# Two depthwise convolutions on one core: where ScalarE issues its four stores among conv 1's images

## The chip, the cores and the metric

The kernel runs on one core of a Trainium2 chip. Its time is the device time of one execution in microseconds, the median of three runs. A core has five engines with a queue of instructions each: TensorE (PE), VectorE (DVE), ScalarE (ACT), GpSimd (POOL) and SyncE (SP). They run side by side and wait for each other through semaphores. Transfers are done by 16 DMA engines, whichever engine issues them. Here SyncE issues loads, ScalarE issues stores and GpSimd and SyncE issue copies within the on-chip memory.

## The reference

```python
def _gn(v, G=32, eps=1e-5):                      # 384 channels in 32 groups of 12
    g = v.reshape(B_, G, C_ // G, H_, W_)
    m = jnp.mean(g, axis=(2, 3, 4), keepdims=True)
    s = jnp.var(g, axis=(2, 3, 4), keepdims=True)
    return ((g - m) / jnp.sqrt(s + eps)).reshape(v.shape)

x = x + depthwise_conv(_gn(x), L0_conv_k)        # 3 x 3, padding 1
w = (w + rot90(w, 1) + rot90(w, 2) + rot90(w, 3)) * 0.25
x = x + depthwise_conv(_gn(x), w)                # 7 x 7, padding 3
```

x is (8, 384, 128, 128) in float32.

## The kernel before

A **unit** is one group of 12 channels of four images, and a **chunk** is four of its channels; three chunks make a unit, and there are 64 units and 192 chunks. The rows of an image lie on the 128 partitions. A chunk passes through a software pipeline: every engine runs `slot(t)` for one t after another, and in a slot it works on several chunks at different stages. The order on each engine is the order in which `slot` is written; only semaphores tie the engines together. Slots repeat in threes, as a unit has three chunks.

In both convolutions, an image is split into a high part and a low part in float16. ScalarE writes the high part of the first normalisation into H1 (L551) and the whole value in float32 into Z (L554), and GpSimd subtracts the one from the other for the low part (L656). TensorE then multiplies with banded matrices (L731), and VectorE adds the result to X and takes its sum (L483). For the second normalisation GpSimd writes the high part into H2 (L635), ScalarE the whole value into the same Z (L534), and VectorE the low part (L466). The rows of H2 have to be gathered into overlapping blocks of rows, BT: GpSimd issues the high gather (L648), SyncE the low one (L238, L240), and VectorE copies the high block once more (L504). TensorE runs conv 2 on BT (L764), and VectorE adds its result to X (L447) and gives `out_done`. ScalarE stores X (L565).

Z has one place for each of four images, and both normalisations use it: L551 of image `img` waits in `normalise1` until L466 has read the older chunk's Z of that image (`lo_done[1]`).

In slot t, ScalarE does in this order: the four L534 of chunk t-4; then L551 and L554 of chunk t+1, image by image, with the store of chunk t-6 of the same image behind each; then `square(t)`, four times L577, which waits for L483 (`y_done`). Only the first of a slot's four stores waits (`out_done`, in `store` with `img == 0`); the others need nothing more. In every third slot TensorE sums over the partitions behind this (L693): it waits for all squares of the unit (`squared`). The sums of the first layer are L703.

VectorE does in slot t: L447 of chunk t-6, the four L466 of chunk t-4, the statistics of a loaded chunk (L475), the four L483 of chunk t, L504 of chunk t-4. SyncE does in slot t: four loads for chunk t+5 (L249), which wait until the store of the chunk that had the place before has landed (`stored`), then eight low gathers for chunk t-4. X holds twelve chunks.

The change touches `slot` of ScalarE only; `store` and `normalise1` are as they were.

Of the kernel before, what the change touches and what calls it, by code (L numbers as in the profile page):

```python
# [13 lines left out]
NI = 4  # L14
# [44 lines left out]
def conv_program(nc, x, k1_in, k2_in, out):  # L59
# [18 lines left out]
    with ExitStack() as ctx:  # L78
# [32 lines left out]
        at = [GC * V1 // 2]  # L111
# [56 lines left out]
        def xs(n, img):  # L168

            c = n % CPU_  # L170
            return X[:, ring(n), c * CC:(c + 1) * CC, img, :]
# [6 lines left out]
        def part(H, n, which, img, off, pitch):  # L178
            return H[:, n % 2, which, :, off + img * pitch:off + img * pitch + W]
# [5 lines left out]
        def walk(eng, slot):  # L185

            for t in range(-5, NCH + 7):
                slot(t, lambda n: n)

        def wait_apart(eng, semaphore, value):  # L190


            eng.wait_ge(semaphore, value)
            if not isinstance(value, int):
                eng.sem_inc(passed, 1)
# [3 lines left out]
        def real(n):  # L199
            return 0 <= n < NCH  # L200
# [321 lines left out]
        @block.scalar  # L522
        def _(act):
            def normalise2(n, at):

                m = NI * at(n)
                rb = RB[:, 1, (n // CPU_) % 2]
                for img in range(NI):

                    if real(n + 4):  # L530
                        act.wait_ge(lo_done[0], m + 4 * NI + img + 1)
                    else:
                        act.wait_ge(lo_done[1], m - NI + img + 1)
                    nc.scalar.activation(Z[:, img, :].rearrange("p (c w) -> p c w", c=CC), xs(n, img),  # L534
                                         ACT.Identity, bias=rb[:, 1, img:img + 1],
                                         scale=rb[:, 0, img:img + 1]).then_inc(normed[1], 1)

            def normalise1(n, img, at):

                m = NI * at(n)  # L540
                rb = RB[:, 0, (n // CPU_) % 2]
                if img == 0:
                    if n == 0:
                        act.wait_ge(zeroed, 9)
                    if n >= 2:
                        wait_apart(act, conv1_done, at(n) - 1)
                if real(n - 5):
                    act.wait_ge(lo_done[1], m - 5 * NI + img + 1)
                elif n > 0:
                    act.wait_ge(lo_done[0], m - NI + img + 1)  # L550
                nc.scalar.activation(part(H1, n, 0, img, O1, P1), xs(n, img), ACT.Identity,  # L551
                                     bias=rb[:, 1, img:img + 1],
                                     scale=rb[:, 0, img:img + 1]).then_inc(hi_done[0], 1)
                nc.scalar.activation(Z[:, img, :].rearrange("p (c w) -> p c w", c=CC), xs(n, img),  # L554
                                     ACT.Identity, bias=rb[:, 1, img:img + 1],
                                     scale=rb[:, 0, img:img + 1]).then_inc(normed[0], 1)

            def store(n, img, at):

                c, half = n % CPU_, (n // CPU_) % HALVES  # L560
                ch0 = (at(n - n % GCH) // GCH) * GC + c * CC
                if img == 0:
                    wait_apart(act, out_done, at(n) + 1)
                dst = out[half * NI + img, bass.ds(ch0, CC), :, :].rearrange("c h w -> h c w")
                act.dma_start(dst, xs(n, img)).then_inc(stored[n % BODY], 16)  # L565

            def take_root(layer, u):
                act.wait_ge(fin[layer], u * FIN + 4)
                nc.scalar.activation(TMP[:, layer, 3], TMP[:, layer, 2], ACT.Sqrt).then_inc(root[layer], 1)  # L569

            def square(n, at):

                for img in range(NI):
                    act.wait_ge(y_done, NI * at(n) + img + 1)
                    if n > 0 or img >= 2:
                        act.wait_ge(squared, NI * at(n) + img - 1)
                    nc.scalar.activation(DUMP[:, img % 2].rearrange("p (c w) -> p c w", c=CC), xs(n, img), ACT.Square,  # L577
                                         accum_out=SS[:, n % CPU_, img, 1:2]).then_inc(squared, 1)

            def slot(t, at):  # L580
                n = t - 4
                if real(n):
                    if n % CPU_ == 0:
                        act.wait_ge(fin[1], (at(n) // CPU_) * FIN + FIN)
                    normalise2(n, at)
                n = t - 3
                if real(n) and n % CPU_ == 0:
                    take_root(1, at(n) // CPU_)
                n = t + 1
                if real(n) and n % CPU_ == 0:  # L590
                    act.wait_ge(fin[0], (at(n) // CPU_) * FIN + FIN)
                for img in range(NI):
                    if real(t + 1):
                        normalise1(t + 1, img, at)
                    if real(t - 6):
                        store(t - 6, img, at)
                if real(t):
                    square(t, at)
                n = t + 2
                if real(n) and n % CPU_ == 0:  # L600
                    take_root(0, at(n) // CPU_)

            walk(act, slot)


# [184 lines left out]
```

## Time and profile before

| | us |
|---|---|
| median of three runs | 3197.03 |
| lowest and highest run | 3193.38, 3197.71 |
| profiled execution, its own time | 3199.24 |
| its span, from the first to the last instruction | 3197.4 |
| TensorE busy in the span | 2858.9 |
| VectorE | 2726.5 |
| GpSimd | 2201.2 |
| ScalarE | 2155.5 |

The profiled execution is one execution. Busy time counts arithmetic only; an issue of a transfer is not in it. In the rows below an engine's name with a q behind it, such as ACTq, means its sequencer, which issues transfers, and PE is TensorE's array. A row's duration of an issue is the time that the sequencer spends on it; the data land later. TensorE's granted clock was 0.968 of full speed in the mean over the span.

### The profile page before, as it was taken

The numbers are of one execution on the slowest core, as the hardware profiler recorded it, in microseconds if no ns is written. First come the engines' busy times: TensorE is split into PE (matmuls) and PEld (weight loads), VectorE is DVE, ScalarE is ACT, GpSimd is POOL, SyncE is SP. The second block draws the span as 40 slices with busy tenths as digits, with TensorE's granted clock in tenths as the row PEclk, the third lists the DMA queues.
The fourth block names the chain that finished last, engine by engine and source line by source line (L and its number), as shares of the span: only waits on it lengthen the run. The fifth ranks groups of instructions, "written<-read, shape, count | busy, mean of one in ns | idle before, by whom it ended". The sixth has DMA issues, their size and how long they took to land.

```text
span 3197.4 us, 76300 instructions
## 1 busy us (share of the span) xinstructions
PE 2858.9 (89%) x28676; PEld 1810.7 (57%) x28676; DVE 2726.5 (85%) x5180; ACT 2155.5 (67%) x3969; POOL 2201.2 (69%) x2321
## 2 busy tenths in 40 slices
PE   0388998999999899999999999999999999989995
PEld 0145565665566565666566666565665565656563
DVE  3377898989899899999899999899898988989885
ACT  1175776777677677777677777677776777767661
POOL 3165776776777677777677777777776777777773
PEclk9798999999999999999999999999999999999997
DMA  2599898888889888989888999888888988988876
GB/s 89 140 234 235 228 237 225 233 225 223 223 237 244 224 223 233 242 234 244 231 233 232 236 234 243 227 232 229 234 231 222 240 236 225 236 229 226 225 181 159
DMA packets 966520, 712.44 MB, mean 223 GB/s; under 512 B 102918, under 2 KB 904710, under 8 KB 966086
## 3 DMA queue, kind: packets, MB, share of 16 engines
q1 hardware_dynamic: 511494, 383.52, 45.8%
q10 hardware_dynamic: 405504, 201.38, 22.5%
q0 software_dynamic: 49152, 122.65, 16.7%
q8 instruction: 227, 3.72, 0.5%
q14 instruction: 143, 1.17, 0.1%
HBM read 259.73 MB, written 220.81 MB: 150 GB/s over the span
## 4 chain that ended last, share of the span: by engine, by line
PE 27%; DVE 23%; POOL 14%; issue 12%; DMA 12%; ACT 5%; SPq 4%; ACTq 2%; DVEq 0%; POOLq 0%
PE PS L731 15%; PE PS L764 11%; POOL H L635 11%; DMA BT<-H 10%; DVE X L483 5%; DVE H L466 5%; DVE BN L475 4%; DVE BT L504 3%; ACT Z L554 2%; ACTq L565 2%; SPq L268 2%; ACT H L551 2%; POOL H L656 2%; POOL BT L648 2%; SPq L238 1%
## 5 line engine op out<-in xcount | busy, mean ns | idle before, releaser
L731 PE MATMUL PS<-H,BAND 128*128 128x512 f16 x6912 | 1567.7, 386 | 78.7 <-DMA BAND<-rows 69.2
L764 PE MATMUL PS<-BT,BAND 118*32 118x512 f16 x21504 | 1277.1, 393 | 129.3 <-issue 98.8
L731 PEld LDWEIGHTS PS<-H,BAND 128*128 128x128 f16 x6912 | 1018.6, 150 | 600.0 <-issue 85.3
L656 POOL TENSOR_TENSOR H<-Z,H 128x512 f16<-128x512 f32 x768 | 840.1, 1096 | 640.7 <-ACT Z L554 639.8
L764 PEld LDWEIGHTS PS<-BT,BAND 118*32 118x32 f16 x21504 | 763.0, 132 | 601.2 <-issue 253.5
L635 POOL TENSOR_SCALAR H<-X,RB 128x512 f16<-128x512 f32 x768 | 894.8, 1174 | 113.3 <-DVE RB L437 78.5
L551 ACT ACTIVATE H<-X,RB 128x512 f16<-128x512 f32 x768 | 619.2, 806 | 436.9 <-DVE H L466 428.5
L554 ACT ACTIVATE Z<-X,RB 128x512 f32<-128x512 f32 x768 | 615.5, 801 | 0.0
L504 DVE COPY BT<-BT 39x8512 f16<-39x8512 f16 x192 | 475.7, 2478 | 161.9 <-DMA BT<-H 158.4
L534 ACT ACTIVATE Z<-X,RB 128x512 f32<-128x512 f32 x768 | 561.4, 803 | 36.2 <-issue 22.0
L577 ACT ACTIVATE DUMP<-X 128x512 bf16<-128x512 f32 x768 | 473.0, 617 | 158.8 <-DVE X L483 156.9
L648 POOL DMA_DIRECT2D BT<-H x768 | 439.1, 577 | 200.2 <-PE PS L764 98.6
L475 DVE BATCH_NORM_STATS2 BN<-X 128x6 f32<-128x512 f32 x768 | 472.5, 675 | 104.9 <-DMA X<-in_x 104.9
L483 DVE SCALAR_TENSOR_TENSOR X<-PS,SC,X 128x512 f32<-128x512 f32 x768 | 528.0, 741 | 30.6 <-PE PS L731 30.3
L466 DVE TENSOR_TENSOR H<-Z,H 128x512 f16<-128x512 f32 x768 | 491.3, 699 | 5.7 <-ACT Z L534 3.4
L447 DVE SCALAR_TENSOR_TENSOR X<-PS,SC,X 128x2048 f32<-128x2048 f32 x192 | 450.2, 2345 | 15.0 <-PE PS L764 12.9
L569 ACT ACTIVATE TMP<-TMP 128x4 f32<-128x4 f32 x128 | 25.6, 200 | 380.6 <-DVE TMP L420 380.6
L577 ACT ACTIVATION_READ_ACCUMULATOR DUMP<-X 128x1 f32 x768 | 143.9, 187 | 0.0
L703 PE MATMUL PS<-MQ,ONES 128*128 128x8 f32 x128 | 25.4, 271 | 64.7 <-DVE MQ L496 64.6
L703 PEld LDWEIGHTS PS<-MQ,ONES 128*128 128x128 f32 x128 | 19.6, 193 | 91.0 <-issue 48.0
L483 DVE DVE_READ_ACCUMULATOR X<-PS,SC,X 128x1 f32 x768 | 61.3, 80 | 0.0
L693 PE MATMUL PS<-SS,ONES 128*128 128x24 f32 x128 | 25.7, 280 | 34.6 <-ACT DUMP L577 34.4
(48 smaller groups left out, 439.6 us busy)
## 6 DMA issues: line engine op xcount, KB each, us to landing
X<-in_x SPq DMA_DIRECT2D x768, 256.0 KB, 5.7
out_y<-X ACTq DMA_DIRECT2D x768, 256.0 KB, 6.7
BT<-H POOLq DMA_DIRECT2D x384, 162.1 KB, 5.2
BT<-H POOLq DMA_DIRECT2D x384, 149.6 KB, 5.6
BT<-H SPq DMA_DIRECT2D x576, 99.8 KB
BT<-H SPq DMA_DIRECT2D x384, 62.3 KB
BT<-H SPq DMA_DIRECT2D x192, 83.1 KB
rows<-v_all SPq DMA_DIRECT2D x8, 1638.0 KB, 11.6
```

Of the source, the lines that this page charges most:

```text
L466: v.tensor_tensor(part(H2, n, 1, img, O2, P2), Z[:, img, :].rearrange("p (c w) -> p c w", c=CC), part(H2, n, 0, img, O2, P2), ALU.subtract ...
L475: v.bn_stats(BN[:, c, img, :], xs(n, img)).then_inc(bn_done, 1)
L483: v.scalar_tensor_tensor(xs(n, img), PA[:, :, img * W:(img + 1) * W], SC[:, 0, bass.ds(g, 1)], xs(n, img), ALU.mult, ALU.add, accum_out=SS ...
L504: v.tensor_copy(BT[AGAIN:AGAIN + WIN, n % 2, :, :, :].rearrange("p b c l -> p (b c l)"), BT[0:WIN, n % 2, :, :, :].rearrange("p b c l -> p ...
L534: nc.scalar.activation(Z[:, img, :].rearrange("p (c w) -> p c w", c=CC), xs(n, img), ACT.Identity, bias=rb[:, 1, img:img + 1], scale=rb[:, ...
L551: nc.scalar.activation(part(H1, n, 0, img, O1, P1), xs(n, img), ACT.Identity, bias=rb[:, 1, img:img + 1], scale=rb[:, 0, img:img + 1]).the ...
L554: nc.scalar.activation(Z[:, img, :].rearrange("p (c w) -> p c w", c=CC), xs(n, img), ACT.Identity, bias=rb[:, 1, img:img + 1], scale=rb[:, ...
L577: nc.scalar.activation(DUMP[:, img % 2].rearrange("p (c w) -> p c w", c=CC), xs(n, img), ACT.Square, accum_out=SS[:, n % CPU_, img, 1:2]). ...
L635: g.tensor_scalar(part(H2, n, 0, img, O2, P2), xs(n, img), rb[:, 0, img:img + 1], rb[:, 1, img:img + 1], ALU.mult, ALU.add).then_inc(hi_do ...
L656: g.tensor_tensor(part(H1, n, 1, img, O1, P1), Z[:, img, :].rearrange("p (c w) -> p c w", c=CC), part(H1, n, 0, img, O1, P1), ALU.subtract ...
L731: last = mm(PA[:, ch, :], band[:, j, ws, :], data[:, :, O1 - 1 + j:O1 - 1 + j + W], start=k == 0, stop=k == 3 * K1 - 1)
L764: last = mm(banks2(n)[b * BL:(b + 1) * BL, ch, :], band[:, j, :], rows, start=j == 0, stop=j == K2 - 1, tile_position=(0, b * BL))
```

## The change

ScalarE no longer issues one store behind each image of conv 1. It issues the stores of images 0 and 1 ahead of the first image, the store of image 2 behind the second image and the store of image 3 behind the fourth.

```diff
@@ -589,11 +589,19 @@
                 n = t + 1
                 if real(n) and n % CPU_ == 0:
                     act.wait_ge(fin[0], (at(n) // CPU_) * FIN + FIN)
-                for img in range(NI):
-                    if real(t + 1):
-                        normalise1(t + 1, img, at)
-                    if real(t - 6):
-                        store(t - 6, img, at)
+                if real(t - 6):
+                    store(t - 6, 0, at)
+                    store(t - 6, 1, at)
+                if real(t + 1):
+                    normalise1(t + 1, 0, at)
+                    normalise1(t + 1, 1, at)
+                if real(t - 6):
+                    store(t - 6, 2, at)
+                if real(t + 1):
+                    normalise1(t + 1, 2, at)
+                    normalise1(t + 1, 3, at)
+                if real(t - 6):
+                    store(t - 6, 3, at)
                 if real(t):
                     square(t, at)
```

ScalarE's queue in one slot before, from the last L534 to the squares. The wait named `lo_done2` is on L466, `out_done` on L447, `y_done` on L483:

```order
L534 ACTIVATE Z<-X,RB 128x512 [waits lo_done1] x3
L551 ACTIVATE H<-X,RB 128x4x128 [waits lo_done2,conv1_done]
L554 ACTIVATE Z<-X,RB 128x512
L565 DMA out_y<-X 128x4x128 [waits out_done]
L551 ACTIVATE H<-X,RB 128x4x128 [waits lo_done2]
L554 ACTIVATE Z<-X,RB 128x512
L565 DMA out_y<-X 128x4x128
L551 ACTIVATE H<-X,RB 128x4x128 [waits lo_done2]
L554 ACTIVATE Z<-X,RB 128x512
L565 DMA out_y<-X 128x4x128
```

Behind it the same three rows come once more for the fourth image, and then the four squares. The same stretch of ScalarE's queue after the change:

```order
L534 ACTIVATE Z<-X,RB 128x512 [waits lo_done1] x3
L565 DMA out_y<-X 128x4x128 [waits out_done]
L565 DMA out_y<-X 128x4x128
L551 ACTIVATE H<-X,RB 128x4x128 [waits lo_done2,conv1_done]
L554 ACTIVATE Z<-X,RB 128x512
L551 ACTIVATE H<-X,RB 128x4x128 [waits lo_done2]
L554 ACTIVATE Z<-X,RB 128x512
L565 DMA out_y<-X 128x4x128
L551 ACTIVATE H<-X,RB 128x4x128 [waits lo_done2]
L554 ACTIVATE Z<-X,RB 128x512
```

The wait for `out_done` and two stores have moved ahead of the first L551; between the second L551 and the third stands one store. The fourth is where it was, ahead of the squares. The order of no other engine changes.

## Rows read from the trace of the kernel before

**Rows 1.** The page's busy times: us busy, share, instructions.

```profile
PE 2858.9 (89%) x28676; PEld 1810.7 (57%) x28676; DVE 2726.5 (85%) x5180; ACT 2155.5 (67%) x3969; POOL 2201.2 (69%) x2321
```

**Rows 2.** Waits of TensorE, 250 to 3120 us: us in total, times, longest.

```profile
PE PS L764 <- issue: 98.8, 31, 13.6
PE PS L693 <- ACT DUMP L577: 29.5, 32, 2.4
PE PS L703 <- DVE MQ L496: 24.1, 19, 2.9
```

**Rows 3.** Chain of waits, 1500 to 1540 us: start, us, what.

```profile
1506.13 5.19 POOL H L635 x4
...
1513.43 9.89 DMA BT<-H
...
1530.13 0.69 DVE H L466
```

**Rows 4.** Timeline of ScalarE: start, us, what, [idle before <- who ended it].

```profile
1526.66 2.93 ACT L534 ACTIVATE Z<-X,RB 128x512 f32<-128x512 f32 x4
1530.93 0.82 ACT L551 ACTIVATE H<-X,RB 128x512 f16<-128x512 f32 x1 [1.34 <-DVE H L466]
1530.98 1.18 ACTq L565 DMA_DIRECT2D out_y<-X  x2
...
1538.95 0.19 ACT L577 ACTIVATION_READ_ACCUMULATOR DUMP<-X 128x1 f32 x1
```

**Rows 5.** Timeline of TensorE, two of its waits.

```profile
1539.19 0.40 PE L693 MATMUL PS<-SS,ONES 128*128 128x24 f32 x2 [1.76 <-ACT DUMP L577]
...
1581.62 8.00 PE L764 MATMUL PS<-BT,BAND 118*32 118x512 f16 x112 [3.39 <-issue]
```

**Rows 6.** Timeline of SyncE ahead of the second of these waits.

```profile
1559.81 7.92 SPq L249 DMA_DIRECT2D X<-in_x  x4
1567.83 0.88 SPq L238 DMA_DIRECT2D BT<-H  x1
...
1575.45 0.71 SPq L240 DMA_DIRECT2D BT<-H  x1
```

**Rows 7.** All instructions of line L565.

```profile
L565 ACTq DMA_DIRECT2D out_y<-X x768: 378/744/4638, 220.9 to 3193.5; - x192
```

**Rows 8.** Timeline of VectorE: the L447 ahead of the L551 above.

```profile
1527.87 2.34 DVE L447 SCALAR_TENSOR_TENSOR X<-PS,SC,X 128x2048 f32<-128x2048 f32 x1
```

**Rows 9.** Timeline of ScalarE: the first two stores of five neighbouring slots.

```profile
1498.10 2.08 ACTq L565 DMA_DIRECT2D out_y<-X  x2
...
1512.01 1.01 ACTq L565 DMA_DIRECT2D out_y<-X  x2
...
1544.50 1.04 ACTq L565 DMA_DIRECT2D out_y<-X  x2
...
1559.03 0.94 ACTq L565 DMA_DIRECT2D out_y<-X  x2
...
1576.41 1.68 ACTq L565 DMA_DIRECT2D out_y<-X  x2
```

**Rows 10.** Timeline of GpSimd behind that slot's images.

```profile
1536.77 1.09 POOL L656 TENSOR_TENSOR H<-Z,H 128x512 f16<-128x512 f32 x1 [0.32 <-ACT Z L554]
1537.84 5.14 POOL L635 TENSOR_SCALAR H<-X,RB 128x512 f16<-128x512 f32 x4
```

**Rows 11.** Waits of VectorE, 250 to 3120 us.

```profile
DVE BT L504 <- DMA BT<-H: 137.2, 81, 4.4
```

**Rows 12.** Table of stretches around two L551; the last but one column is DMA share.

```profile
1511.30:1512.70 1.40, 1.40 (x8) 0.98 (x7) 1.40 (x3) 0.74 (x2) 0.83 (x3) 1.00 0.69 192
1530.20:1531.60 1.40, 1.40 (x17) 0.74 (x19) 1.40 (x4) 0.67 (x1) 0.00 (x0) 1.00 0.87 167
```

**Rows 13.** Waits of ScalarE, 250 to 3120 us.

```profile
ACT H L551 <- DVE H L466: 423.4, 183, 5.8
```

## The prediction

> **What bounds the kernel now.** I read the page's busy times first, then the waits of each engine in the steady part (250 to 3120 us), then the chain of waits over one group of channels, then the timeline of ScalarE where the change is. TensorE is busy 89% of the span [rows 1]; in the steady part its waits come to some 150 us: 98.8 us ahead of conv 2 in 31 places, 29.5 us ahead of the layer-2 sums (L693) in 32 places, 24.1 us ahead of the layer-1 sums (L703) in 19 [rows 2]. The steady part has 61 groups of three chunks, so the L693 wait is there in about half of them. An edit that touches only ScalarE's order can act through these waits and nothing else.
>
> Who sets the L693 wait is seen in the chain [rows 3]. VectorE makes the scale and shift of a unit, GpSimd makes four high parts (L635, 5.19 us), the high gather takes 9.89 us, VectorE copies it (L504), adds conv 2 of an older chunk (L447), makes the low parts (L466), and the first of these frees ScalarE's buffer Z for the first image of conv 1 (L551 at 1530.93). From there ScalarE has eight activations and four squares without a gap: the last accumulator is read at 1538.95 and done at 1539.14 [rows 4], and TensorE, which had idled 1.76 us, starts L693 at 1539.19 [rows 5]. So 8.2 us of ScalarE lie on that path, and a delay of L551 there goes to TensorE one for one whenever the wait is there at all. The 3.39 us ahead of conv 2 at 1581.62 [rows 5] have another cause: SyncE's four loads took 7.92 us to issue from 1559.81, its eight low gathers came only behind them, from 1567.83 to 1576.16 [rows 6], and conv 2 began 5.5 us after the last.
>
> Where the stores stand in this is the point of the case. Today the first two stores are issued from 0.05 us behind the start of L551, not ahead of it: 1530.98, for 1.18 us [rows 4]. During that the activation engine works on what is already queued, so the issue costs nothing, however long. It is often long: 378 ns at least, 744 ns in the median, 4638 ns at most [rows 7].
>
> **The change, part by part.** The number of stores, their bytes and every engine's arithmetic stay. Four things move.
>
> (1) Two stores stand ahead of L551. They wait for `out_done`, which L447 gives at its end, 1530.21 [rows 8]; at this time ScalarE's four L534 are over (1529.59) and its queue is empty [rows 4], so nothing covers the issue. L551 today starts at 1530.93, 0.72 us behind L447. After the change it needs the wait to pass, both issues, and its own dispatch. For wait and dispatch I take 0.15 us, an estimate from the 0.05 us between L551 and the first issue and the 0.11 us between the end of L466 and L551 [rows 3, 4]. For the pair of issues I take what it takes today, in six neighbouring slots: 1.18 us [rows 4] and 2.08, 1.01, 1.04, 0.94 and 1.68 us [rows 9], mean 1.32. The delay of L551 is then 0.15 + 1.32 - 0.72 = 0.75 us, with 0.37 us from the shortest pair and 1.51 us from the longest as bounds. It goes to the path in the 32 places where L693 waits: 32 x 0.75 = +24 us (bounds 12 and 48). In the other groups TensorE comes later than ScalarE, and the delay falls into that slack. So it does in the two slots of a group that have no L693 behind them: TensorE's list names ScalarE at L693 alone [rows 2], since the images that these slots prepare feed a conv 1 that comes a slot later.
>
> At this place a rule of the Trainium skill speaks against my term. The row says that the issue holds ScalarE's sequencer 744 ns in the median [rows 7]. The Trainium skill, page "DMA: Bandwidth & Descriptors", section "Issuing engines are not separate DMA queues", says that the sequencer's time to initiate a DMA "is usually small relative to the DMA itself". By the rule the pair ahead would cost next to nothing, and the sum would lose its first two terms and be -12 us, 3185 us; by the row it keeps them. I go by the row, and the short issue is a rival below.
>
> (2) GpSimd's low parts (L656) follow ScalarE image by image, and the next chunk's L635 starts right behind the last of them (1536.77 + 1.09, L635 at 1537.84) [rows 10]. So the next high gather is issued 0.75 us later too. VectorE waited for a gather's landing in 81 places [rows 11], so a part of them passes the delay on, and TensorE sees it at L703 in 19 places. At most 19 x 0.75 = 14 us, at least nothing; I take a third, +5 us, since only every third gather is of this kind.
>
> (3) The first two stores start some 0.65 us earlier, as L447's end stands 0.72 us ahead of L551. That uses DMA time which is free: the 16 DMA engines are busy 0.69 in the 1.4 us around one such start and 0.87 around another [rows 12]. In the slot whose gather lies on the chain the free share is 0.31, so the saturated stretch behind it becomes 0.65 x 0.31 = 0.2 us shorter. 32 x 0.2 = -6 us; bounds are nothing and the whole shift, 32 x 0.65 = -21 us.
>
> (4) SyncE's loads and low gathers meet the stores 0.65 us earlier. Where the loads are late, as at 1559.81, the stores have gone a little further and the loads come through sooner; where they were early, they now overlap with two stores. 31 stalls, at 0.2 us each as in (3), -6 us; the bounds are the whole shift either way, -20 and +20 us.
>
> The third store is issued behind four dispatched activations and the fourth behind eight, as far into ScalarE's queue as today or earlier. At its place the third store has three activations waiting, some 2.1 us, and the one that runs, 0.8 us (L551's duration in [rows 4]), to hide in; only an issue of over 2.5 us would starve the engine. I cost it at nothing; without the cover it would be some tenths in the few longest cases.
>
> Sum: 24 + 5 - 6 - 6 = +17 us on the profiled execution, whose own time is 3199.24 us: 3216. The median of the runs shown is 3197.03, 2.2 us below the profiled one, so I predict 3214 us.
>
> **Rivals.** *Nothing to be measured.* The time that TensorE loses at L693 is won back by the other waits: while TensorE idles, the DMA engines catch up, gathers land sooner, and the 98.8 us ahead of conv 2 shrink. For this speaks that the DMA engines are nearly full, so every added pause gives them room, and that a shorter pair (0.94 us as in [rows 9]) leaves a first term of 12 us, which (3) and (4) cancel: 12 + 0 - 6 - 6 = 0, 3197 us. Against it: the gather on the chain was issued before the pause, so the pause can't help it.
>
> *Faster.* The stores' start is what matters, not L551: with 1 MB of stores 0.65 us ahead, the high gather on the chain and the low gathers both land 0.65 us sooner (the bounds of 3 and 4), -21 and -20 us, and the first term is at its lower bound: 12 - 21 - 20 = -29 us at the extreme. With three quarters of the shift won it is 12 - 16 - 15 = -19 us, 3178 us, which I take as this rival's time. For it speaks that the gather's 9.89 us are the longest single piece of the chain [rows 3]. It decides from the point where more than the first term's 12 us come back, which is over a quarter of the shift in (3) and (4) together; that the DMA engines are 0.69 and 0.87 busy there already [rows 12] speaks against it.
>
> *A short issue.* If the pair takes no more than 0.57 us at its new place, it fits between L447 and L551 (0.15 + 0.57 = 0.72), terms 1 and 2 are nothing, and -6 - 6 = -12 us are left: 3185 us. The shortest issue is 378 ns [rows 7], so two of them take 0.76 us at least, and L551 would still be 0.19 us late; that speaks against.
>
> *The change doesn't do what it says.* If `out_done` came so late that the stores ahead held ScalarE for it, L551 would wait for VectorE once more. It can't: L447 is ahead of L466 on VectorE, and L551 waits for L466 already. If it came long before, the stores would be issued under the idle time ahead of L551 (423.4 us in 183 places [rows 13]); then nothing is delayed. L447's end only 0.72 us ahead of L551 excludes that in this slot.
>
> **How the numbers follow.** Forecast, slower by some 17 us: 0.60. Nothing to be measured: 0.21. Faster by the earlier start: 0.13, by a short issue: 0.04. The last 0.02 are for something slower still by other ways. What a measurement of this kernel can tell from no change is about 0.2%, 6.4 us. The bounds of term 1 with the likely others give the likeliest case's own range, 3202 to 3238. The second case is at 3197, and most of the third has to be in as well if no more than 2 in 10 is to be left out, so the range is 3180 to 3240.
>
> **What would show it.** In the profile of the changed kernel the first L565 of a slot should start at the end of L447, L551 should start 1.1 to 2.2 us behind L447 instead of 0.7, and ScalarE's idle time ahead of L551 should be put down to something else than L466. From L551 to L693 it should still be 8.2 us where TensorE waits. The wait ahead of L693 should grow from 29.5 us to over 45 us, and in more places than 32; TensorE's clock should hold. If the pair of issues takes under 0.6 us at its new place, step 1 is wrong. If L693 waits more and the wait ahead of conv 2 falls by as much, the first rival holds; if L504 waits much less for its gather, the second.

## The result and the profile after

| | before | after |
|---|---|---|
| median, us | 3197.37 | 3273.64 |
| lowest and highest run | 3193.38, 3230.71 | 3268.19, 3280.61 |
| profiled execution, its own time | 3199.24 | 3268.19 |

The changed kernel is slower by 76 us by the medians. The ratio over all runs is 1.021, with a 95% interval of 1.0168 to 1.0252; it stands for some 67 us, since it counts the run of before that took 3230.71 us. Ratios and differences here and below leave out two slow runs, one of 7537.16 us in e3_third_slots and one of 3228.63 us of the kernel before. The direction was forecast, the size was not: 17 us were forecast, and 3273.64 lies outside the range of 3180 to 3240.

TensorE's waits in the steady part of the changed kernel (250 to 3190 us), to be read beside [rows 2]: us in total, times, longest. L701, L772 and L711 are what was L693, L764 and L703.

```profile
PE PS L701 <- ACT DUMP L577: 122.9, 56, 4.0
PE PS L772 <- issue: 34.3, 9, 13.4
PE PS L711 <- DVE MQ L496: 28.2, 24, 4.1
```

The wait ahead of the layer-2 sums is up by 93 us and stands in nearly every group of three chunks; the wait ahead of conv 2 is down by 64 us. An "issue" wait is one whose end the profile puts down to nothing that it shows; ahead of conv 2 the prediction tied it to SyncE's loads and low gathers. All waits of this view sum to 159 us before and 196 us after, so they explain 37 of the 69 us by which the two profiled executions differ. Most of the rest is TensorE's busy time, which rises from 2858.9 to 2888.1 us, by 29 us. The page's costliest groups show where, first before, then after (busy us and mean ns behind the first bar):

```profile
L731 PE MATMUL PS<-H,BAND 128*128 128x512 f16 x6912 | 1567.7, 386 | 78.7 <-DMA BAND<-rows 69.2
L764 PE MATMUL PS<-BT,BAND 118*32 118x512 f16 x21504 | 1277.1, 393 | 129.3 <-issue 98.8
```
```profile
L739 PE MATMUL PS<-H,BAND 128*128 128x512 f16 x6912 | 1615.7, 394 | 86.1 <-DMA BAND<-rows 69.0
L772 PE MATMUL PS<-BT,BAND 118*32 118x512 f16 x21504 | 1249.7, 387 | 63.5 <-issue 34.3
```

Conv 1 takes 48 us more and conv 2 27 us less.

One third slot of the changed kernel, first VectorE and ScalarE, then TensorE, beside [rows 4, 5, 8] (start, us, what, idle before):

```profile
1559.27 2.34 DVE L447 SCALAR_TENSOR_TENSOR X<-PS,SC,X 128x2048 f32<-128x2048 f32 x1
```
```profile
1561.70 1.44 ACTq L565 DMA_DIRECT2D out_y<-X  x2
1563.24 0.82 ACT L551 ACTIVATE H<-X,RB 128x512 f16<-128x512 f32 x1 [2.26 <-DVE H L466]
...
1571.28 0.19 ACT L577 ACTIVATION_READ_ACCUMULATOR DUMP<-X 128x1 f32 x1
```
```profile
1571.52 0.62 PE L701 MATMUL PS<-SS,ONES 128*128 128x24 f32 x2 [2.82 <-ACT DUMP L577]
1571.96 9.36 PE L739 MATMUL PS<-H,BAND 128*128 128x512 f16 x36
```

The steps are as forecast: L447 ends at 1561.61, the two stores are issued from 1561.70 to 1563.14, and L551 starts at 1563.24, 1.63 us behind L447 instead of 0.72. From L551 to the last accumulator it is 8.2 us as before. TensorE idles 2.82 us, and then conv 1 takes 9.36 us instead of the usual 8.03. In the table of stretches (length in us, TensorE busy, granted clock, DMA share, GB/s) that conv 1 is seen to start at half the clock:

```profile
1571.90:1573.60 1.70, 1.70 (x6) 0.50 0.49 108
1573.60:1576.00 2.40, 2.40 (x10) 0.76 0.82 204
```

The granted clock is 0.50, the lower of the two levels (1.2 of 2.4 GHz), behind a pause, and 1.00 from 1576.00 us on. There are 64 conv 1 that open a unit: the kernel's first, which took over 9 us in every run, and 63 behind layer-2 sums. Of the 64, 6 took over 9 us before and 32 after; their time above the usual 8.03 us is 11 us before and 59 us after. So 37 us more of waits and 29 us more of busy time (48 us of it more in conv 1, 27 us less in conv 2) make up 66 of the 69 us between the two profiles.

### The profile page after: what moved, and what is told of

Read it like the earlier page. It is cut to its first block, busy times and chain, and to the rows that moved or that the text cites. A ratio compares the mean times of both kernels' runs of the same rounds, so it can differ in the third digit from the quotient of the medians.

```text
span 3266.3 us, 76361 instructions
## 1 busy us (share of the span) xinstructions
PE 2888.1 (88%) x28676; PEld 1804.9 (55%) x28676; DVE 2765.6 (85%) x5180; ACT 2151.2 (66%) x3969; POOL 2201.5 (67%) x2321
## 4 chain that ended last, share of the span: by engine, by line
DVE 28%; PE 16%; DMA 15%; POOL 15%; ACT 10%; issue 9%; ACTq 4%; SPq 2%; POOLq 0%; DVEq 0%
DMA BT<-H 14%; PE PS L739 13%; POOL H L643 11%; DVE X L483 6%; DVE BT L504 5%; DVE X L447 4%; ACT Z L554 4%; ACTq L565 4%; ACT H L551 4%; DVE H L466 3%; DVE BN L475 3%; PE PS L772 3%; POOL BT L656 2%; SPq L268 2%; ACT DUMP L577 2%
## 5 line engine op out<-in xcount | busy, mean ns | idle before, releaser
L739 PE MATMUL PS<-H,BAND 128*128 128x512 f16 x6912 | 1615.7, 394 | 86.1 <-DMA BAND<-rows 69.0
L664 POOL TENSOR_TENSOR H<-Z,H 128x512 f16<-128x512 f32 x768 | 911.9, 1190 | 745.3 <-ACT Z L554 744.0
L772 PE MATMUL PS<-BT,BAND 118*32 118x512 f16 x21504 | 1249.7, 387 | 63.5 <-issue 34.3
L772 PEld LDWEIGHTS PS<-BT,BAND 118*32 118x32 f16 x21504 | 746.7, 131 | 523.1 <-issue 158.3
L551 ACT ACTIVATE H<-X,RB 128x512 f16<-128x512 f32 x768 | 619.0, 806 | 576.1 <-DVE H L466 534.8
L643 POOL TENSOR_SCALAR H<-X,RB 128x512 f16<-128x512 f32 x768 | 813.6, 1068 | 115.2 <-DVE RB L437 103.5
L504 DVE COPY BT<-BT 39x8512 f16<-39x8512 f16 x192 | 490.7, 2556 | 172.8 <-DMA BT<-H 169.5
L554 ACT ACTIVATE Z<-X,RB 128x512 f32<-128x512 f32 x768 | 615.6, 802 | 0.0
L534 ACT ACTIVATE Z<-X,RB 128x512 f32<-128x512 f32 x768 | 561.7, 803 | 41.3 <-issue 22.7
L483 DVE SCALAR_TENSOR_TENSOR X<-PS,SC,X 128x512 f32<-128x512 f32 x768 | 528.7, 744 | 68.9 <-PE PS L739 68.1
L656 POOL DMA_DIRECT2D BT<-H x768 | 448.7, 590 | 162.3 <-POOL H L643 86.5
L466 DVE TENSOR_TENSOR H<-Z,H 128x512 f16<-128x512 f32 x768 | 491.9, 700 | 7.6 <-ACT Z L534 4.8
L447 DVE SCALAR_TENSOR_TENSOR X<-PS,SC,X 128x2048 f32<-128x2048 f32 x192 | 450.2, 2345 | 14.1 <-PE PS L772 12.0
L701 PE MATMUL PS<-SS,ONES 128*128 128x24 f32 x128 | 29.3, 310 | 128.2 <-ACT DUMP L577 128.1
L701 PEld LDWEIGHTS PS<-SS,ONES 128*128 128x128 f32 x128 | 22.4, 219 | 157.6 <-ACT DUMP L577 156.4
L711 PE MATMUL PS<-MQ,ONES 128*128 128x8 f32 x128 | 25.8, 274 | 69.1 <-DVE MQ L496 68.9
L711 PEld LDWEIGHTS PS<-MQ,ONES 128*128 128x128 f32 x128 | 20.0, 197 | 95.9 <-DVE MQ L496 49.8
```

Of the source, the lines that this page charges most:

```text
L447: v.scalar_tensor_tensor(y, banks2(n).rearrange("p b w -> p (b w)"), SC[:, 1, bass.ds(g, 1)], y, ALU.mult, ALU.add).then_inc(out_done, 1)
L466: v.tensor_tensor(part(H2, n, 1, img, O2, P2), Z[:, img, :].rearrange("p (c w) -> p c w", c=CC), part(H2, n, 0, img, O2, P2), ALU.subtract ...
L483: v.scalar_tensor_tensor(xs(n, img), PA[:, :, img * W:(img + 1) * W], SC[:, 0, bass.ds(g, 1)], xs(n, img), ALU.mult, ALU.add, accum_out=SS ...
L504: v.tensor_copy(BT[AGAIN:AGAIN + WIN, n % 2, :, :, :].rearrange("p b c l -> p (b c l)"), BT[0:WIN, n % 2, :, :, :].rearrange("p b c l -> p ...
L643: g.tensor_scalar(part(H2, n, 0, img, O2, P2), xs(n, img), rb[:, 0, img:img + 1], rb[:, 1, img:img + 1], ALU.mult, ALU.add).then_inc(hi_do ...
L664: g.tensor_tensor(part(H1, n, 1, img, O1, P1), Z[:, img, :].rearrange("p (c w) -> p c w", c=CC), part(H1, n, 0, img, O1, P1), ALU.subtract ...
```

## The experiments

Each run has its ratio to runs of the kernel before on the same chip. The medians of before were between 3197 and 3209 us on these chips, so ratios are compared, not medians. "Late" is the distance from the end of L447 to the start of L551 in the third slots, the ones with L693 behind their squares; it is 0.71 us in the mean before and 2.01 us after. The 95% intervals reach 0.2 to 0.5% to either side. The profile of a run is one execution, while single executions of the kernel before lay between 3179 and 3231 us, so small differences between two profiles say little.

| run | ratio | 95% interval | late, third slots | conv 1 over 9 us, of 64 |
|---|---|---|---|---|
| the change | 1.021 | 1.0168 to 1.0252 | 2.01 | 32 |
| e1_one_ahead | 1.0114 | 1.0075 to 1.0152 | 0.70 | 9 |
| e2_none_ahead | 1.0096 | 1.0059 to 1.0132 | 0.72 | 14 |
| e3_third_slots | 1.0101 | 1.0066 to 1.0137 | 2.07 | 28 |
| e4_other_slots | 1.0119 | 1.0084 to 1.0154 | 0.72 | 10 |
| e5_delay_0_7 | 1.0038 | 1.0015 to 1.0061 | 1.42 | 12 |
| e6_delay_1_4 | 1.0166 | 1.013 to 1.0201 | 2.13 | 39 |
| e7_filled_pause | 1.022 | 1.0185 to 1.0255 | 2.04 | 10 |
| e14_delay_filled | 1.0124 | 1.0079 to 1.0169 | 2.13 | 13 |
| e8_filled_before | 1.0021 | 0.9985 to 1.0057 | 0.72 | 2 |
| e9_later_stores | 0.9921 | 0.9898 to 0.9944 | 0.72 | 4 |
| e12_later_one_slot | 0.9926 | 0.989 to 0.9963 | 0.72 | 6 |
| e13_ahead_one_slot | 1.0044 | 1.002 to 1.0069 | 0.72 | 11 |
| e11_all_last | 0.9764 | 0.973 to 0.9798 | 0.72 | 4 |
| e16_last_two_slots | 0.9781 | 0.9735 to 0.9826 | 0.72 | 3 |
| e15_behind_squares | 0.9887 | 0.9854 to 0.9921 | 0.72 | 2 |

### Taking the change apart

Theory A was that of the prediction: the issues ahead of L551 make ScalarE late, and that counts in the third slots only. Theory B was that the earlier transfers cost by themselves. The orders below are of one slot; n is an image (L551 and L554), s a store.

```diff
 before              n0 s0 n1 s1 n2 s2 n3 s3
 the change          s0 s1 n0 n1 s2 n2 n3 s3
+e1_one_ahead        s0 n0 s1 n1 s2 n2 n3 s3
+e2_none_ahead       n0 s0 s1 n1 s2 n2 n3 s3
+e3_third_slots      the change where t % 3 == 2, before elsewhere
+e4_other_slots      before where t % 3 == 2, the change elsewhere
```

> Only the first store stands ahead of L551, the other three follow images 0, 1 and 3 at the places they had before (behind the first, the third and the fourth image, with one behind the first). Theory A (the two issues hold ScalarE's sequencer, L551 starts late in the slot with L693 behind it): one issue of 0.38 to 0.45 us plus some 0.2 us fits into the 0.71 us between L447 and L551, so no delay and no change: 3190 to 3203 us, L551 still 0.7 us behind L447. Theory B (the earlier transfers themselves crowd the gathers): about half of the 76 us, 3225 to 3245 us.

The text is wrong in its first bracket: the other three stores stand behind the first, second and fourth image, as in the diff. Measured: ratio 1.0114, +1.1%. L551 is not late (0.70 us), and the run is slower all the same; its median of 3246.47 us is just above what B expected. The lateness of L551 alone, as theory A had it, isn't the whole cause. The first store starts 0.7 to 0.9 us earlier here than before, the second 0.5 us.

> Two stores directly behind the first image, none ahead of it, the third behind the second image's place in the queue and the fourth last. Theory A: L551 isn't delayed, 3190 to 3203 us. Theory B (bunched stores are what costs): most of the 76 us stay, over 3240 us.

Here store 1 stands right behind store 0, and store 2 behind the second image. Measured: +1.0%, L551 not late. This falls between the two expectations: not nothing, not most of the loss.

This run hardly moves a store in time. Behind the start of L551 the first starts 0.06 us in the mean as before, the second 0.48 instead of 0.57 us, the third 1.5 us in both. What it changes is the cover: while both issues run, ScalarE has the two activations of the first image and no more, and it runs dry. ScalarE's waits between images (250 to 3050 us) show it, first the kernel before, then e2:

```profile
ACT H L551 <- issue: 5.6, 10, 0.9
```
```profile
ACT H L551 <- issue: 61.4, 74, 2.9
```

In the third slots the stretch from the first L551 to the last square is 8.56 us in the mean and not 8.19, and the wait at L693 is 60.7 us and not 29.1. So e2 shows again that an uncovered issue costs time, and it says nothing of an earlier start. How much of its 1.0% this is wasn't measured apart. In e1 the same row has 16.2 us, so a small part of e1's 1.1% may be of this kind too.

> The changed order only in every third slot, the one with L693 behind its squares; the order of before in the other two. Theory A: nearly the whole loss, 3255 to 3275 us, with L693's wait over 100 us and over 25 conv 1 at the lower clock. Theory B: a third of the loss, 3215 to 3230 us.

> The changed order in the two slots of a group that have no L693 behind them; the order of before in the third. Theory A: L551 is late there by some 0.5 us and slack takes it: 3195 to 3210 us. Theory B: two thirds of the loss, 3240 to 3255 us.

Measured: +1.0% and +1.2%, 33 and 40 us on that chip. The two halves add up to the whole. Theory A had neither right: the third slots give less than it wanted, and the other two, where it saw slack, give more than half. Theory B had the other two slots right (3248.91 us) and the third too low. In the third-slot run (TensorE's waits, 250 to 3050 us) the mark of A is all there, in the other there is little of it:

```profile
PE PS L693 <- ACT DUMP L577: 102.2, 52, 3.4
PE PS L764 <- issue: 47.5, 17, 11.5
```
```profile
PE PS L764 <- issue: 91.7, 19, 12.9
PE PS L693 <- ACT DUMP L577: 53.6, 38, 2.5
```

So the loss has two parts, one in the third slots and one in the other two. In e4 two things change in those other slots: the stores start earlier, and L551 is later (1.39 and 1.31 us behind L447 instead of 0.69 and 0.90). No run has that lateness alone in these slots.

### The delay alone

```diff
 if real(t + 1):
+    if img == 0 and t % 3 == 2 and real(t - 4):
+        act.wait_ge(lo_done[1], NI * at(t + 1) - 5 * NI + 1)
+        for pad in range(2):
+            nc.scalar.activation(PAD[:, pad].rearrange("p (c w) -> p c w", c=CC), xs(t + 1, img), ACT.Identity,
...
     normalise1(t + 1, img, at)
 if real(t - 6):
     store(t - 6, img, at)
```

The diff is the run with 1.4 us; the one with 0.7 us has one activation and not two.

> The order of stores of before; in the third slot of each group ScalarE does one activation more, on a tile of its own, between the wait of the first L551 and L551 itself, so that all eight activations and the squares behind it come 0.7 us later and no transfer is moved by choice. The delay alone, by the places: 0.7 us at L693, each pause of over 1.3 us there followed in part by a conv 1 of 9.7 us instead of 8.0. If the delay ahead of L693 is what cost the changed kernel its 30 to 40 us of the third slots: 3215 to 3235 us beside 3200 to 3209 for before. If those 30 to 40 us come from the transfers: within 6 us of before.

> As the run with 0.7 us, with two such activations, 1.4 us, which is about the mean delay that the changed kernel has there (2.01 less 0.71 us behind L447). If the delay ahead of L693 is the cause in the third slots: 30 to 50 us over before, with L693's wait near 105 us and 25 or more conv 1 at the lower clock, as in the run with the changed order in the third slots alone. If the transfers are: within 6 us of before.

Measured: +0.4% (12 us) and +1.7% (54 us). The delay alone is enough to cost what the third slots cost, and more: e3, with nearly the same lateness (2.07 and 2.13 us), has +1.0%. The first 0.7 us are cheap, the second are not. With 0.7 us the time was in the range expected for the delay as the cause, with 1.4 us it was 4 us above it. Why e3 costs less than e6 stays open (the two intervals just overlap); its stores of the third slot start earlier, which may help there, but no run has that alone. TensorE's waits in the run with 1.4 us (250 to 3180 us) have the pattern of the changed kernel, more at L693 (here L700) and less at conv 2 (here L771):

```profile
PE PS L700 <- ACT DUMP L578: 113.0, 54, 3.9
PE PS L771 <- issue: 43.2, 20, 9.6
```

### The clock behind the pause

```diff
-pe.wait_ge(squared, NI * at(u) + NI * CPU_)
 pe.wait_ge(y_done, NI * at(u) + NI * CPU_)
+for _ in range(10):
+    mm(PS[:, CC - 1, 128:384], ONES1[:].bitcast(F16)[:, 0:P], ONES1[:].bitcast(F16), start=True, stop=True)
+pe.wait_ge(squared, NI * at(u) + NI * CPU_)
```

> The changed kernel, and TensorE does ten matmuls on a constant tile (128 x 256 columns each, about 0.11 us, so 1.1 us) between conv 2 and the wait of L693; they write columns that L739 of the next chunk starts anew. If the slow conv 1 behind L693 (32 of some 62) are the clock falling in the pause, few are left and the time falls by 20 to 45 us, to 3230 to 3255 us. If the 1.7 us have another cause, the time stays or rises by up to 10 us.

> The kernel before with the same ten matmuls ahead of L693's wait as in the filled-pause run. It measures what the filling costs by itself where hardly a conv 1 was slow (6 of 64). If it costs nothing, 3197 to 3212 us; then the 42 us that fewer slow conv 1 freed in the filled changed kernel were taken by other waits, and the clock is no cause of its own. If the filling costs 1.1 us in the groups where TensorE comes later than ScalarE, 20 to 45 us over before; then the filled changed kernel did gain by the clock about as much as it lost by the filling.

> The run with 1.4 us of delay in the third slots and TensorE's ten matmuls ahead of L693's wait. If the 39 slow conv 1 of the delay run cost their 1.7 us each on the path, the time falls from 3260 to 3205 to 3235 us. If other waits take what they free, as the filled changed kernel suggests, 3250 to 3270 us.

The filling itself costs nothing that can be told (e8, interval 0.9985 to 1.0057). It does to the clock what it should: slow conv 1 fall from 32 to 10 in the changed kernel, from 39 to 13 in the delay run. But the time hardly follows. The changed kernel stays where it was (1.022 beside 1.021), though the conv 1 that open a unit take some 42 us less. TensorE's waits in e7 (250 to 3180 us) show in part where they went; L774 is conv 2:

```profile
PE PS L774 <- issue: 50.4, 13, 7.3
PE PS L703 <- ACT DUMP L577: 41.0, 41, 2.4
```

The wait ahead of conv 2 is 50.4 us and not 34.3, that ahead of the layer-1 sums 34.4 and not 28.2, and conv 2 itself is busy for 17 us more (1266.7 beside 1249.7 us). In the delay run the filling took 0.4%, some 13 us, off the time (1.0124 beside 1.0166), with intervals that overlap; its median is between the two expectations. So in one pair the filling gains nothing and in the other some 13 us, and neither difference is clear of the noise. The slow matmuls are in the main a mark of the pause; what they cost on top of it is small here and not settled, and the 48 us more of conv 1 in the profile are not a price.

### When the stores start

Theory C took the place of B: in the two other slots the high gather, which the chain of waits runs through, is issued close to the stores, and stores that start earlier would take DMA time from it.

```diff
 before              n0 s0 n1 s1 n2 s2 n3 s3
+e9_later_stores     n0 n1 s0 n2 s1 n3 s2 s3
+e12_later_one_slot  the same where t % 3 == 1, before elsewhere
+e13_ahead_one_slot  s0 s1 n0 n1 s2 n2 n3 s3 where t % 3 == 1, before elsewhere
+e11_all_last        n0 n1 n2 n3 s0 s1 s2 s3
+e16_last_two_slots  the same where t % 3 != 2, before elsewhere
+e15_behind_squares  n0 n1 n2 n3, the four squares, s0 s1 s2 s3
```

> Against the change: the order on ScalarE is image 0, image 1, store 0, image 2, store 1, image 3, store 2, store 3, so that every store starts some 0.6 to 1.4 us later than before and none is ahead of an image. Theory C (stores that start earlier take the DMA engines from the high gather, issued about when L551 starts): high gather and L504 come sooner, 3165 to 3190 us. If the gathers don't mind, 3195 to 3210 us. If stores are late for the loads that wait for their place, 3215 us or more, with more of SyncE's wait for stores than 66 us.

Measured: -0.8%, 24 us faster.

> The later order (image 0, 1, store 0, image 2, store 1, image 3, store 2, store 3) only in the slot of a group in which the high gather of the chain is issued beside the stores; the order of before in the other two. If that gather is what the earlier or later start acts through: most of the gain of the run with later stores everywhere, 12 to 28 us under before. If it acts in every slot alike: a third of it, 5 to 10 us.

> The changed order (two stores ahead) only in that same slot. L551 is late there by 0.4 us, and slack of over 1 us stands behind it. If the stores' earlier start slows the gather of the chain: 20 to 40 us over before, as in the run with the changed order in two slots. If not: within 10 us of before.

Measured: later in the one slot gives -0.7%, as much as later everywhere. Ahead in the same slot gives +0.4% (18 us by the medians), just under the 20 us that C expected at least; L551 is late there too, by 1.28 us instead of 0.90, so a part of the 18 us may be that. So this slot counts. Whether it does so through the high gather is less plain. VectorE's waits for gathers (250 to 3050 us) are 135.6 us in the kernel before. The extremes are these, first e13, then e11 (all four stores last, below):

```profile
DVE BT L504 <- DMA BT<-H: 169.4, 80, 5.2
```
```profile
DVE BT L504 <- DMA BT<-H: 104.1, 66, 5.3
```

In e1, with one store ahead in every slot, it is 171.0 us. But it is 129.4 us in e12, only 6 us under before, in a run that gained 22 us; it is 142.7 us in the changed kernel and 152.0 us in e4, which have two stores ahead in the same slot as e13. And in runs with the stores in the places of before it is anything from 119.1 us (e8) to 153.2 us (e5). The gather's own time gives no better measure. From its issue to L504 in the slots with t % 3 == 1 it is 10.2 us in the mean before, 9.9 in e11, 10.9 in e13 and 11.0 in e1, but 10.2 in e12 as well, and 10.6 both in the changed kernel and in e6, where no store was moved. These figures go with theory C for the largest shifts, and they don't show it.

> All four stores behind the fourth image. Theory C (the later the stores, the freer the gather on the chain): at or below the run with later stores, 3165 to 3185 us. If SyncE's loads then wait for their place, or the squares behind a long issue come late: 3190 to 3225 us, with more of SyncE's wait for stores than 66 us or with L693's wait over 40 us.

Measured: -2.4%, 3132.49 us beside 3203 us, 33 us under the lowest time that C gave. This is the best of all orders with e16, and faster than both kernels of the case. The high gather can't be all of it: in the slots with t % 3 == 1 it is shorter by 0.3 us in 64 groups, some 18 us of 71. The largest difference in TensorE's waits (250 to 3050 us) is ahead of conv 2, where the kernel before has 98.8 us:

```profile
PE PS L764 <- issue: 41.9, 17, 13.1
```

In e16 it is 36.0 us and in e12 74.1 us. The prediction tied this wait to SyncE's loads and low gathers, which share the DMA engines with the stores as the high gather does. No run tells the two apart.

> All four stores behind the fourth image in the two slots without L693, the order of before in the third. If the earlier and later start act through the gathers of those two slots (0.3 us each between a gather's issue and L504): 3135 to 3155 us, most of the gain of the run with all stores last. If every slot gives a like share: about 3150 to 3160 us; if the third slot gives most: over 3170 us.

Measured: -2.2%, 3128.69 us beside 3198.73 us, better than expected and within the intervals the same as with the stores last in all slots. So the later start of the stores acts in the two slots without L693, and the third hardly cares.

> All four stores behind the four squares, two to three us later than in the run with all stores last. If later is still better: under 3122 us. If SyncE's loads now wait too long for their place, or the issues delay the next chunk's L534: 3130 to 3190 us, with SyncE's wait for stores over 200 us.

Measured: -1.1%, in the middle of the expectation: the gain of e11 is half lost. SyncE's waits for stores (250 to 3050 us) show the other end of the trade, first e11, then e15:

```profile
SPq L249 <- DMA out_y<-X: 168.5, 76, 7.9
```
```profile
SPq L249 <- DMA out_y<-X: 372.5, 129, 10.3
```

and with it TensorE's wait ahead of conv 2 (here L767), since SyncE's low gathers stand behind the loads:

```profile
PE PS L767 <- issue: 124.3, 47, 12.1
```

In e15 VectorE's wait for gathers is down to 64.0 us and L693's to 10.5 us, the lowest of all runs without the filling, and conv 2 waits the most. Of the places tried the best is the one between, behind the fourth image.

## Why the prediction was right in direction and wrong in size

**Step 1, the two stores ahead.** The mechanism was right: stores start at L447's end, L551 waits for both issues, nothing covers them. The size was not. The price was taken as 0.75 us in 32 places. The mean lateness in the third slots is 2.01 us, so the delay is 2.01 - 0.71 = 1.30 us. The pair of issues takes 1.81 us there in the mean; the six neighbouring slots gave 1.32, but mixed the three kinds of slot, and over all third slots of the kernel before it was 1.44. And the wait stands in 56 places, not 32: a delay of 1.3 us also uses up the slack of groups that had some. Counting only the places that wait already took the slack to be larger than the delay. By experiment the third slots cost 33 us (e3), and the delay alone 54 us (e6); the forecast had 24.

**The rule of the Trainium skill.** The Trainium skill's page "DMA: Bandwidth & Descriptors" (section "Issuing engines are not separate DMA queues") has initiating a DMA as usually small relative to the DMA. Taken by its words the trace agrees: an issue takes 0.744 us in the median, and the store lands 6.7 us behind its issue in the median. What doesn't follow is that it costs next to nothing, and there the row decided rightly: the pair at 1561.70 took 1.44 us of ScalarE's sequencer with nothing to cover it.

**Steps 3 and 4, the earlier start of the stores.** These are the terms that failed, by their sign. They were booked as a gain of 12 us, 6 for the gather on the chain and 6 for SyncE, because the DMA engines had a free share at the start. The runs have the opposite sign: with L551 on time, stores that start 0.5 to 0.9 us earlier cost 1.1% (e1; a part of it is ScalarE running dry, 16.2 beside 5.6 us), and later ones gain 0.7 to 2.4% (e9, e12, e11, e16). That the start of the stores in the two slots without L693 matters, and that later is better up to the fourth image, is shown. ScalarE running dry can't be what the later stores save, since the kernel before has only 5.6 us of it. Through which transfer the start acts, the high gather or SyncE's loads and low gathers, is not shown. Of SyncE's half of the step the wait for stores tells: it is 65.8 us before and 64.8 us after (250 to 3050 us), so the earlier stores freed no place for a load sooner.

**Step 2, the later gather.** It was forecast to be seen at the layer-1 sums, with 5 us; their wait went from 24.1 to 28.2 us.

**The third and fourth store** were costed at nothing. ScalarE's eight activations stay without a gap in the changed kernel, so for ScalarE that holds. But as transfers they moved too: counted from the end of L447 they start 0.7 to 1.2 us earlier in the two slots without L693, and 0.2 us earlier in the third. That belongs to the same term as step 3; its share wasn't measured apart.

**What was left out.** The prediction had TensorE's waits as the only way for the edit to act, and its clock was expected to hold. TensorE's busy time rose by 29 us, and 32 conv 1 were slow instead of 6. As e7 and e14 show, this is in the main a mark of the pauses, not a price that comes on top.

**The rivals.** "Nothing to be measured" had the right mechanism in part: the wait ahead of conv 2 did shrink, by 64 us, against 93 us more at L693. In 250 to 3050 us it is low where L551 is late in the third slots (e6 43.2, e3 47.5 us) and hardly lower than the 98.8 us of before where it is on time there and stores start earlier (e1 96.5, e4 91.7 us). That fits what this rival said, that a pause gives the transfers time. "Faster" was the mirror image of what happened; it spoke of 1 MB of stores ahead, while step 3 moved two of the four stores, 0.5 MB. The likeliest case was too small because its two gains were no gains and its delay was priced too low: with the measured halves, 33 us for the third slots and 40 us for the others, the sum is 73 us. The direction was right for the reason given in step 1, but by e3 that step is about half of the loss; for the other half the prediction had the opposite sign.

## What to carry to other kernels

A transfer's place in an engine's queue is its start in time. Try the stores later, as late as the loads that reuse their buffer allow: here that is worth 2.4%, and one step further half of it is lost. An issue is free only behind enough queued work: it was covered behind the images one by one, ScalarE ran dry when two issues followed two activations (e2), and at the head of an idle queue it is paid in full. Price a delay against the slack of the places that don't wait yet as well: the first 0.7 us cost 12 us here, the second 42 us. And when matmuls take longer behind a pause, look at the pause first: bringing most of them back to their usual time gave little or nothing.

## What the runs showed of the hardware

The first store of a slot is issued in 0.38 to 0.45 us in nearly every slot of the kernel before (at most 0.64 us), the second takes 0.84 us in the mean and up to 3.3 us. The two move the same bytes, so here the sequencer's time for a store went with what was issued shortly before it. At the head of the queue this stayed so; in the third slots the pair took 1.81 us in the mean, in the other two slots of a group 1.04 and 1.13 us.

Whether TensorE's clock is low behind a pause at L693 doesn't follow from the length of that pause alone. In the kernel before, a pause of 1.34 us is followed by a conv 1 of 9.72 us, and one of 2.44 us by a conv 1 of 8.03 us. Ten short matmuls ahead of the wait kept most conv 1 at their usual 8.03 us (10 slow of 64 instead of 32), and the time hardly moved.
